# A chunked RWKV-7 scan block: its token operations placed anew and cut in number, its values copied by SBUF-to-SBUF DMA, its value-key products made on POOL

## What is computed

```python
def step(state, inp):
    r_t, d_t, k_t, v_t, a_t, b_t = inp
    sa = jnp.einsum('bhij,bhj->bhi', state, a_t)
    state = state * d_t[:, :, None, :] + sa[..., None] * b_t[:, :, None, :] + v_t[..., None] * k_t[:, :, None, :]
    return (state, jnp.einsum('bhij,bhj->bhi', state, r_t))
```

## Time and profile before

| what | value |
|---|---|
| median of 3 runs | 1334.06 us (1333.65 to 1337.86) |
| the profiled execution | 1342.32 us, its span 1340.8 us |
| first scan step, last scan step | 68.1 us, 1248.6 us |
| PE, DVE, ACT, POOL busy | 1109.0, 980.0, 707.1, 614.5 us |

### The profile page before, as it was taken

One profiled execution on the slowest core, in us unless ns is written; L12 is line 12 of the kernel. 1 busy time (PEld: TensorE's weight loads), 2 busy tenths in 40 slices (PEclk: granted clock), 3 DMA queues, 4 the chain that ended last, 5 costly groups with the idle time before them and its releaser, 6 DMA issues.

```text
span 1340.8 us, 18152 instructions
## 1 busy us (share of the span) xinstructions
PE 1109.0 (83%) x4819; PEld 568.4 (42%) x4819; DVE 980.0 (73%) x2368; ACT 707.1 (53%) x1087; POOL 614.5 (46%) x869
## 2 busy tenths in 40 slices
PE   3576767988988987988888987898889888889896
PEld 1233334444444444444444444444344444444332
DVE  2367786879798786979688895979688797967311
ACT  1534455556565545656365555656365665634454
POOL 0145454455555554555455453555455554555200
PEclk9867688899999998999899998999899999999998
DMA  2000000000000000000000000000000000000000
GB/s 105 0 9 1 16 0 17 1 17 1 24 1 24 1 12 14 8 16 0 24 0 23 1 8 16 0 24 0 24 0 8 16 16 0 1 16 17 0 8 16
DMA packets 7442, 16.35 MB, mean 12 GB/s; under 512 B 956, under 2 KB 956, under 8 KB 7240
## 3 DMA queue, kind: packets, MB, share of 16 engines
q1 hardware_dynamic: 7368, 15.58, 3.4%
HBM read 11.38 MB, written 4.19 MB: 12 GB/s over the span
## 4 chain that ended last, share of the span: by engine, by line
PE 38%; DVE 37%; issue 18%; ACT 4%; DMA 1%; DVEq 1%; SPq 0%; POOL 0%; ACTq 0%; POOLq 0%
DVE state L903 7%; PE sa_ps L365 7%; DVE upd L899 6%; PE fin_a L542 5%; PE pre_b L312 4%; PE pre_a L312 3%; PE mid_ps L312 3%; DVE s_a L889 3%; PE vb_ps L312 3%; DVE kv L877 2%; PE fin_b L542 2%; PE mid_ps L496 2%; PE fin_a L312 2%; DVE y L1051 2%; PE pre_a L424 1%
## 5 line engine op out<-in xcount | busy, mean ns | idle before, releaser
L1099 POOL TENSOR_TENSOR plus_kv<-state,kv 128x128 f32<-128x128 f32 x512 | 284.4, 555 | 575.7 <-DVE state L903 537.9
L365 PE MATMUL sa_ps<-s_a,con 128*128 128x128 f32 x1024 | 240.9, 319 | 150.9 <-DVE s_a L889 144.6
L365 PEld LDWEIGHTS sa_ps<-s_a,con 128*128 128x128 f32 x1024 | 181.2, 202 | 431.1 <-DVE s_a L889 374.1
L899 DVE TENSOR_TENSOR upd<-sa_ps,b_t 128x128 f32<-128x128 f32 x512 | 145.3, 284 | 168.9 <-PE sa_ps L365 168.2
L1092 POOL TENSOR_TENSOR s_r<-state,r_t 128x256 f32<-128x256 f32 x256 | 217.8, 851 | 1.0 <-DVE state L903 1.0
L903 DVE TENSOR_TENSOR state<-upd,plus_kv 128x128 f32<-128x128 f32 x512 | 153.6, 300 | 17.7
L889 DVE TENSOR_TENSOR s_a<-state,a_t 128x128 f32<-128x128 f32 x512 | 149.7, 292 | 19.0 <-DVE state L903 1.3
L542 PE MATMUL fin_b<-h_e,mat 128*128 128x512 f32 x256 | 131.1, 610 | 11.7 <-ACT pick L777 11.0
L542 PE MATMUL fin_a<-h_e,mat 128*128 128x512 f32 x256 | 122.1, 593 | 0.0
L345 PE MATMUL vb_ps<-con,val_rep 128*128 128x128 f32 x512 | 84.6, 291 | 13.9 <-ACT val_rep L597 7.7
L877 DVE TENSOR_TENSOR kv<-vb_ps,k_t 128x512 f32<-128x512 f32 x128 | 87.5, 684 | 1.8 <-PE vb_ps L345 1.6
(11 more groups left out here) (191 smaller groups left out, 2050.9 us busy)
## 6 DMA issues: line engine op xcount, KB each, us to landing
x_in<-xT SPq DMA_DIRECT2D x16, 256.0 KB, 2.7
x_res<-xT SPq DMA_DIRECT2D x16, 256.0 KB, 2.8
outT<-res SPq DMA_DIRECT2D x16, 256.0 KB, 2.0
mat<-mats SPq DMA_DIRECT2D x1, 2306.0 KB
con<-consts SPq DMA_DIRECT2D x1, 584.0 KB, 3.5
hid<-b SPq DMA_DIRECT2D x3, 8.0 KB
vec<-vecs SPq DMA_DIRECT2D x1, 11.5 KB, 3.5
```

The lines of the kernel that those rows point to most:

```text
L365: mm(sa_ps[:, 0:STATE], k("sum8"), s_a[:], start=True, stop=True).then_inc(s["sa"], 1)
L899: tt(ib(upd[:]), ib(sa_ps[:, 0:STATE]), over_i(b_t[c.slot][:, t * B:(t + 1) * B]), ALU.mult).then_inc(s["upd"], 1)
L1099: tt(plus_kv[:, (t % 2) * STATE:(t % 2 + 1) * STATE], st(t), kv[:, at:at + STATE], ALU.add).then_inc(s["plus_kv"], 1)
```

## The change

A table `AT` gives the step of every token operation, counted from the first scan step of its own chunk: -32 to -1 lies in the frame before, 32 to 63 in the one after, 64 to 91 in the second after. The frames go from -1 to 17. An engine that takes no part in the scan (ACT, SP) uses the same numbers only as an order.

Values: `v` is one matmul of 512 columns with the values of a head's channel i on 16 partitions, ACT copies it to `val_c`, and SP issues eight DMAs for each quarter; each copies 16 partitions of 128 columns (512 bytes) to eight partitions each. POOL then makes `kv` in four pieces of 256 columns a quarter, one in each odd step, after its `plus_kv`.

Fewer operations: the mixes for `w1` and `a1` go into the weights (two matmuls of 128 output rows on the present and on the past tokens), `dec` and the second norm's two scaled copies are made on ACT and `kf` is then one sum, the lower bound of the key norm is put into `kk`, `rkb` is made on POOL (with `r_k` in a constant), `x1_keep`, `o_sb` and `lvar` are gone. `tables` loads a table where the one needed isn't the last one loaded. Eleven small constants are new.

```diff
+AT = {
+    "c0": -32, "x_in": -29, "sq0": -28, "j0": -23, "rs0": -22, "x1": -21, "xh0": -20, "c1": -20, "sq1": -20,
+    "j1": -19, "rs1": -17, "xh1": -17, "xn": -15, "dx": -15, "wa": -14, "mix_r": -14, "mix_k": -13, "k": -13,
+    "th_w": -12, "mix_v": -12, "key": -12, "w2": -12, "th_d": -12, "val_c": -11, "mix_g": -11, "rk": -11,
+    "v": -10, "kks": -10, "k2": -10, "val_sb": -10, "p": -10, "val": -9, "cum": -9, "rep": (-9, 11, 12, 15),
+    "r": -8, "rec": -8, "g1": -8, "kk": -8, "rkb": -7, "k_t": -7, "kki": -7, "a_t": -7, "rkb_ps": -5,
+    "th_g": -4, "r_t": -4, "bonus": -4, "g2": -1, "b_t": 0, "bonus_b": 0, "gate": 1, "gsq": 29, "grs": 33,
+    "x_res": 36, "gj": 36, "gxh": 39, "gaff": 41, "gg": 41, "wo": 42, "x2": 43, "fc": 43, "fsq": 43,
+    "x2x": 44, "fj": 44, "frs": 45, "fxh": 46, "xf": 48, "kf": 48, "f1": (48, 49, 49, 55),
+    "hid": (49, 49, 49, 54), "f2": (53, 54, 55, 57), "y1": 57, "ec": 57, "esq": 58, "ej": 58, "ers": 59,
+    "h": 60, "router": 60, "pick_sb": 60, "best": 61, "onehot": 61, "masks": 61, "h_e": (62, 63, 65, 66),
+    "pick": 63, "moe": (64, 65, 65, 66, 67, 69, 69, 70, 71, 72, 72, 73, 74, 77, 79, 79),
+    "act": (64, 72, 73, 80), "y1b": 77, "mo": (78, 80, 83, 84), "lsq": 84, "y2": 86, "lj": 88, "lrs": 88,
+    "store": 88, "lxh": 90, "res": 91,
+}
+FIRST, LAST = -1, CHUNKS + 1
...
             def iteration(c):
                 for t in range(STEPS):
...
+                        for skew in range(-FIRST, CHUNKS - LAST - 2, -1):
+                            if (c + skew).has():
+                                work(c + skew, t - skew * STEPS)
...
+            def replicate(c, q):
...
+                if not isinstance(free, int) or free > 0:
+                    sp.wait_ge(s["kv"], free)
+                sp.wait_ge(s["val_c"], now)
+                for i in range(N):
+                    heads = val_c[i * H:(i + 1) * H, q * QCOLS:(q + 1) * QCOLS].unsqueeze(1).broadcast_to([H, N, QCOLS])
+                    sp.dma_start(val_rep[slot][:, i * QCOLS:(i + 1) * QCOLS], heads).then_inc(s[f"val_rep{slot}"], 16)
...
+                if at == AT["wa"]:
+                    pe.wait_ge(s["xn"], c.count())
+                    pe.wait_ge(s["xh1"], c.count())
+                    mm(pre_a[:], w("w1"), xn[c.slot][:, B:B + COLS], start=True, stop=False)
+                    mm(pre_a[:], wa_past[:], xn[c.slot][:, 0:COLS], start=False, stop=True).then_inc(s["wa"], 1)
...
+                if at == AT["v"]:
+                    pe.wait_ge(s["mix_v"], c.count())
+                    pe.wait_ge(s["th_d"], c.count())
+                    one(pre_a[:], val_scan[:], mix["v"][:], "v")
...
+            def tables(name):
+
+                if loaded[0] != name:
+                    nc.scalar.preload_act_table_set(name)
+                    loaded[0] = name
...
+                    f(dec_bt[:], dec_bt[:], ACT.Identity, bias=half_col[:], scale=0.5).then_inc(s["dec"], 1)
...
+                    f(val_c[:], pre_a[:], ACT.Identity).then_inc(s["val_c"], 1)
...
+                    f(xf_past[:, B:B + COLS], y_m[:], ACT.Identity, bias=past_b[:], scale=past_w[:]).then_inc(s["xf_past"], 1)
+                    f(xf_now[:], y_m[:], ACT.Identity, bias=now_b[:], scale=now_w[:]).then_inc(s["xf_now"], 1)
...
+                    stt(kk[:], rs_p[:], 1e12, key[:], ALU.min, ALU.mult).then_inc(s["kk"], 1)
...
+                    tt(kf[:], xf_now[:], xf_past[:, 0:COLS], ALU.add).then_inc(s["kf"], 1)
...
+            def spread_kv(c, q, part):
+
+                if part == 0:
+                    pool.wait_ge(s["k_t"], c.count())
+                if part in (0, 2):
+                    pool.wait_ge(s[f"val_rep{q % 2}"], c.count(16 * N * (q // 2 + 1), 32 * N))
...
+                tt(to, values, keys.unsqueeze(1).broadcast_to([128, 2, QUARTER, B]), ALU.mult).then_inc(s["kv"], 1)
...
+                q, part = divmod(t, QUARTER)
+                nxt = (c, q + 1) if q + 1 < QUARTERS else (c + 1, 0)
+                if part % 2 == 1 and nxt[0].has():
+                    spread_kv(*nxt, part // 2)
...
+                    tt(rkb[:], rec[:], k2[:], ALU.mult).then_inc(s["rkb"], 1)
```

More of the change, by code:

```diff
@@ L170, in build @@
         th_w, low_a = low[0:DW, :], low[DW:2 * DW, :]
-        rkb, kk, kki, inv_p, th_a = mix["w"], mix["a"], mix["g"], dec_bt, dx
+        rkb, kk, kki, inv_p, th_a = mix["k"], mix["v"], mix["g"], dec_bt, dx
         rec = sb("rec", COLS)
@@ L202, in build @@
         names = """x_in x_res stored consts_in w_in consts_ready
[L203 to L207, removed]
+            wo_turned wo_sb wo_c wv_turned wv_sb wv_c bo_c c0 sq0 j0 ln0 rs0 xh0 x1 c1 sq1 j1 ln1 rs1 xh1 xn carry dx mix_k mix_v mix_r mix_g
+            wa th_w low_a k key v val_c val_rep0 val_rep1 val_mm val r rec g1 th_g w2 th_d dec a2 th_a cum p inv_p
+            sqk kks lnk rk kk kki b_t a_t ka_f k2 k_t r_t rkb rkb_ps bonus bonus_b g2 gate
+            state s_a sa plus_kv upd kv s_r o
+            gsq gj gln grs gxh gaff gg wo x2 x2x fc fsq fj fln frs fxh xf_now xf_past fcarry kf
             f1 relu hid
             f2 y1 y1b ec esq ej eln ers h router best eq score best2 onehot masks h_e pick_ps pick moe act
-            mo y2 lsq lj lvar lln lrs lxh res""".split()
+            mo y2 lsq lj lln lrs lxh res""".split()
         s = {n: sem("s_" + n) for n in names}
@@ L258, in pipeline @@
                     iteration(Chunk(first, n))
-            for c in range(LOOP_START + RING * loops, CHUNKS + 3):
+            for c in range(LOOP_START + RING * loops, LAST + 1):
                 iteration(Chunk(0, c))
-            finish()
-        last_pre = CHUNKS - 1
         @block.sync
         def _(sp):
[L268 to L286, removed]
-                sp.wait_ge(s["w_in"], 64)
[L288 to L304, removed]
@@ L337, in spread @@
[L337 to L347, removed]
+            pe.wait_ge(s["consts_in"], 32)
@@ L817, in _ @@
+            pipeline(nc.scalar, work)
         @block.vector
@@ new lines, in work @@
+                if at == AT["onehot"]:
+                    dve.wait_ge(s["score"], c.count())
+                    nc.vector.tensor_reduce(best2[:], rows(score), AX.X, ALU.max).then_inc(s["best2"], 1)
+                    dve.wait_ge(s["best2"], c.count())
+                    if c.has(1):
+                        dve.wait_ge(s["pick_ps"], (c + -1).count())
+                    for n in range(3):
+                        to = onehot[:].rearrange("p (n r) -> p n r", r=PICKS)[:, :, 32 * n:32 * n + E]
+                        tt(to, rows(score), every(best2), ALU.is_equal).then_inc(s["onehot"], 1)
@@ L1069, in _ @@
+            pipeline(nc.vector, work, scan_step)
         @block.gpsimd
@@ L1142, in fin @@
[L1142 to L1153 removed]
+                others()
```

1368 lines of the change are left out of this document (633 added, 735 removed).

## The result

The changed kernel takes 1263.7 us (median of four runs, 1262.5 to 1265.8) against 1336.0 for the kernel before on the same chip: 0.946 of its time, 95% interval 0.9435 to 0.9486. It is faster, by 72 us where I forecast 105 to 107. The time lies in the forecast range and 35 us above the forecast value. The profiled execution took 1263.8 us, its span 1261.6.

The account below looks back on a forecast made before the run. It took the kernel before as DVE-bound with PE close behind. 14.5 frames x 5.9 = 85.5, plus 18.6 (tail) and 1 (head), 105.1 off 1342.3, left 1237.2; median 8.3 lower, 1229 us; own range 1195 to 1265, wide range 1175 to 1300.

Parts of the forecast that it names:

- the waits' case: Rival, chance 0.16: handovers between PE, ACT and DVE in steps 9 to 17 cost 2.5 to 5 us a frame; 1265 to 1315.
- the frame's sum: Each step priced as the largest of round trip 1.52, DVE's operations and PE's matmuls; 65.5 us over 32 steps.
- Frame after, 67.3: Step prices 65.5 plus contention 1.5 plus waits 0.3 give 67.3 us a frame, 5.9 less than 73.2.
- DVE's savings: DVE's token work per frame falls by 10.5 us, from 62.1 to 51.6, of which kv is 5.5.
- PE's savings: PE loses 32 transposes a frame, 3.4 us, and pays about 0.8 for the second wa matmul.
- Contention, 1.5 a frame: POOL's pieces slow two-input DVE operations: 0.4 each for dx, mix_g and step 25's key products, 0.3 for res.
- Copies, zero: Quarter 0's eighth copy lands 6.7 us after first issue, when POOL wants it; cost zero, upper bound 4.9 a frame.
- Jump, kept at 7.5: The loop's jump, four times in the run, stays at 7.5 us each; if doubled, 30 us would come back.
- Head and tail: Before the first step 1 us less (bounds +4, -4); after the last step 18.6 less (bounds 12 and 24).
- Contention as the bound: Rival, chance 0.05: two-input DVE operations slowed by POOL cost 6 us a frame; about 1315, with POOL's backlog 1345.
- late copies: Rival, chance 0.04: POOL waits in step 25 with the next plus_kv queued behind, the scan stops; slower, 1340 to 1380.
- Tighter packing: Rival, chance 0.10: lagging lanes hide 1.5 us, contention costs nothing, frame 64; 1150 to 1185, 1195 at its upper edge.

Follow-up runs that it names:

- experiment 1: Changed kernel plus three 512-column matmuls a chunk, results unread, in PE's gaps (steps 28, 29, 30): 1228.4 us.
- experiment 2: Changed kernel plus three unread matmuls at steps 28, 29, 30, with only 16 columns instead of 512: 1261.7 us.
- experiment 5: Changed kernel with the kv pieces made on DVE instead of POOL, in the same odd steps: 1262.0 us.
- experiment 6: Changed kernel with each kv piece on POOL cut to 32 of its 256 columns, leaving out seven eighths of the value-key products: 1243.7 us.
- experiment 7: Changed kernel with three unread 512-column matmuls a chunk, all frames written out without hardware loop, and kv pieces on DVE: 1219.5 us.
- experiment 4: Changed kernel with three unread 512-column matmuls a chunk and all frames written out without hardware loop: 1212.0 us.

## Why the prediction was right, and where its sizes were not

That 1263.7 fell into the range of my own case (1195 to 1265), by 1.3 us, is luck. The frames missed by some 45 us, and the jumps, which the sum left as they were, gave 19 back; without that the time would have been near 1282, in the range of the waits' case.

The step that failed is the frame's sum, which prices every step at PE's full clock and adds to that "no more than 0.3 a frame" for waits. What stands in its place is 2.8 us a frame of low clock in steps 30, 31, 0 and 1. I had counted 0, 0, 0 and 1 matmuls in steps 28 to 31 and priced these steps by DVE and by the round trip at full clock. The windows show a clock of 0.98 before, and I read it as given; it depends on what the placing leaves to PE. Shown by experiments 1 and 2: with work in the gaps 1228.4 us and a frame of 67.3, with the same instructions but almost no work in them 1261.7. The TensorE page of the Trainium skill ("TensorE: Matmul & The Clock Gate", "HAM oscillation — how this bites in real kernels") warns of idle gaps of PE. The trace agrees that gaps came before the fall; here they were several short ones, none longer than 1.12 us in the stretch shown.

**Frame after, 67.3.** With the clock kept the count is met, but partly by errors that cancel. The printed step prices add up to 28.8 and 36.3, 65.1 together (not 65.5), and the measured 67.3 includes all contention. Step 22 is 1.3 shorter than priced, 15, 19, 24 and 26 about 0.6 each; 12, 20, 21, 28 and 10 are 0.6 to 0.8 longer. Step 25 is the longest, with 4.6 us (4.3 priced).

**DVE's savings.** "DVE loses kv, 5.5 us" is right as busy time and worth little as time: moving the pieces to POOL gave nothing at the low clock (1262 and 1264) and 7.5 us, half a microsecond a frame, at the full one. On either engine they cost 18 to 20 us (experiments 5 and 6). With the pieces on DVE (experiment 7 against 4) step 9 is 0.85 longer and steps 1, 7, 15, 17 and 31 about 0.25 each, but step 10 is 0.95 shorter; the other odd steps stay within 0.2. **PE's savings** (3.4 a frame) measured 2.6 to 3.0. That is the part of the change in kv's way that pays. How the rest divides between the new steps and the other operations that are gone was not taken apart.

**Contention, 1.5 a frame.** The pieces cost 1.25 (experiment 6). The mechanism is another than the one that I named: in the changed kernel `dx` and `k_t` take 0.70 and 0.69 us in the median, less than before. Instead POOL's operations hold `s_a` and the state update, 4.4 us in the frame shown.

**Copies, zero.** Landing 7.0 against 6.7, each copy 2.4 from issue to landing where I took 2.7; cost 0.2 a frame. That POOL waits for the DMA in each frame (16 waits) is one of the signs by which I called the prediction wrong. It came true and decided nothing.

**Jump, kept at 7.5.** It fell to 2.8. DVE's idle time at it fell from 3.8 to 2.7; at the old jump PE was left idle for 5.1 us, and its next matmul (507.41 on its timeline) took 1.92 us at low clock. In the changed kernel the clock is low at that place anyway. Experiments 1 and 4 agree: with the clock kept, frames 1 to 14 lose 18.0 us when they are written out, 4.5 a jump. The rest of the old price was not taken apart. 18.8 us came from here, which hid over a third of the frames' shortfall.

**Head and tail.** 4.7 against 1, 0.7 beyond the bound of 4. The first feed-forward matmul of chunk 15 starts at 1209.8, to set beside the earlier trace rows: 25.3 us after the last step instead of 22, gain 15.1, within 12 to 24. With the clock kept the tail takes 72.9 us (73.6 forecast).

**Rivals.** Waits: the nearest to what happened (its 1265 to 1315 begins 1.3 above the measured time), but not in steps 9 to 17 and not by the wait itself. Contention as the bound and late copies did not come: POOL's wait is 1.6 to 2.4 us a frame after the first, and the scan sees about 0.2 of it. Tighter packing did not come either: the fastest complete version takes 1212.0, above its 1195.

## What to carry to other kernels

When work is placed anew, look at what is left to PE in each stretch: here a serial chain gathered into steps without matmuls lowered the granted clock for the steps after it, and three matmuls that nobody reads, in gaps where PE waits anyway, brought 35 us of 1264. Busy time taken from an engine isn't time: 5.5 us a frame moved from DVE to POOL were worth 0.5 at most, since on POOL they cost nearly as much time (experiments 5 to 7), while 3.4 taken off PE were worth 2.6 to 3.0. And a loop's jump is worth measuring once with the frames written out (14 us here, 16 with the clock kept).

## What was not expected of the hardware

A scan instruction of DVE with two SBUF inputs that starts beside a POOL operation lasted until 0.13 to 0.15 us after POOL's end, in all 161 cases of the trace where that had more than 0.2 us left (up to 1.25 us for 0.29 of work), so a short instruction on the scan's path can cost as much as the long one beside it. Four DMA issues placed in ACT's order took it 2.77 us. The granted clock fell to 0.50 after a stretch in which no gap of PE was longer than 1.12 us, and stayed there for 9.5 us, although PE was busy for 8.3 of them.
